# Two of eight tiles of an 8-bit rounding step finished on GpSimd instead of VectorE

## What is computed

```python
def _fp8_matmul(x2d, w):
    scale_x = jnp.maximum(jnp.max(jnp.abs(x2d)) / FP8_MAX, 1e-06)
    scale_w = jnp.maximum(jnp.max(jnp.abs(w)) / FP8_MAX, 1e-06)
    x8 = (x2d / scale_x).astype(jnp.float8_e4m3fn)
    w8 = (w / scale_w).astype(jnp.float8_e4m3fn)
    out = jnp.matmul(x8.astype(x2d.dtype), w8.astype(x2d.dtype).T)
    return out * (scale_x * scale_w)
h = _fp8_matmul(x2d, w_fc)               # 1024 x 1024
h = jnp.square(jax.nn.relu(h))
out = _fp8_matmul(h, w_proj)             # the second product; its h is rounded here
...
x = x + _L0_xattn_ref(_layernorm(x), ctx_512, ...)
x = x + _L0_ffn_ref(_layernorm(x), L0_ffn_w_fc, L0_ffn_w_proj)
x = x + _L1_xattn_ref(ctx_512, ctx_512, mask_SxS2_bk1, mask_BxS2_bf0, _layernorm(x), ...)
x = x + _L1_ffn_ref(_layernorm(x), ...)
```

## Time and profile before

| | |
|---|---|
| median of 3 runs | 506.76 us (506.63 to 507.72) |
| the profiled execution, whole time | 507.15 us |
| the profiled execution, from first to last instruction (its span) | 505.4 us |
| TensorE busy | 408.4 us, 81% of the span |
| VectorE busy | 353.0 us, 70% |
| ScalarE busy | 230.5 us, 46% |
| GpSimd busy | 201.5 us, 40% |
| TensorE's mean granted clock | 0.916 of 2.4 GHz |
| the chain that ended last | TensorE 54%, VectorE 26%, issue 7%, ScalarE 7%, GpSimd 4%, DMA 2% |

### The profile page before, as it was taken

How to read it: one execution, slowest core, us unless ns; L and a number is a source line. 1 busy time by engine, 2 the same in 40 slices (tenths; PEclk the granted TensorE clock), 3 DMA queues, 4 the chain that set the end, 5 groups by cost and what they waited for, 6 DMA issues and landing times.

```text
span 505.4 us, 5862 instructions
## 1 busy us (share of the span) xinstructions
PE 408.4 (81%) x1900; PEld 299.5 (59%) x1901; DVE 353.0 (70%) x765; ACT 230.5 (46%) x562; POOL 201.5 (40%) x150
## 2 busy tenths in 40 slices
PE   2956997999897988998989999929645058969997
PEld 2735776777786877777767888613423044524465
DVE  4996869868779699697786626474699966582322
ACT  1432653756666657666566550135792123311100
POOL 2582642644545627555566449771001110040000
PEclk9976999999999999999999999965895577979999
DMA  8633020020100200000200012000000000000011
GB/s 324 211 102 148 1 84 0 1 84 3 44 40 0 85 1 1 0 2 8 108 1 0 2 50 99 1 0 1 0 0 0 1 1 0 0 1 1 0 42 42
DMA packets 8941, 18.82 MB, mean 37 GB/s; under 512 B 2128, under 2 KB 6672, under 8 KB 7760
## 3 DMA queue, kind: packets, MB, share of 16 engines
q1 hardware_dynamic: 8912, 18.46, 10.6%
HBM read 17.40 MB, written 1.05 MB: 37 GB/s over the span
## 4 chain that ended last, share of the span: by engine, by line
PE 54%; DVE 26%; issue 7%; ACT 7%; POOL 4%; DMA 2%; SPq 0%; POOLq 0%; DVEq 0%; ACTq 0%
PE bank L1191 10%; PE bank L1196 5%; PE bank L1380 5%; PE bank L1398 5%; PE bank L1179 4%; PE bank L1090 4%; PE bank L1092 4%; PE bank L1091 4%; PE bank L1166 3%; POOL rot_low L387 2%; DVE negmax L806 2%; DVE tail_all L1011 2%; PE bank L1296 2%; PE bank L1085 2%; DVE qr L751 2%
## 5 line engine op out<-in xcount | busy, mean ns | idle before, releaser
L392 POOL TENSOR_TENSOR prob<-prob,rinv 128x512 f32<-128x512 f32 x64 | 77.0, 1203 | 104.5 <-DVE rinv L811 104.4
L549 ACT ACTIVATE prob<-bank,negmax 128x256 f32<-128x256 f32 x128 | 59.6, 470 | 53.2 <-DVE negmax L806 53.0
L1191 PE MATMUL bank<-probT,kva 128*128 128x256 f32 x256 | 68.2, 388 | 14.1 <-ACT probT L540 13.5
L1191 PEld LDWEIGHTS bank<-probT,kva 128*128 128x128 f32 x256 | 46.4, 189 | 27.9 <-ACT probT L540 20.8
L806 DVE TENSOR_REDUCE negmax<-bank 128x2 f32<-128x512 f32 x64 | 43.9, 685 | 18.3 <-PE bank L1166 18.2
L365 POOL TENSOR_TENSOR c_y<-c_ve,minus_half 128x4 f32<-128x4 f32 (+1 forms) x10 | 12.4, 1244 | 101.7 <-DVE c_ve L686 76.3
L540 ACT COPY probT<-bank 128x512 f32<-128x512 f32 x64 | 37.7, 588 | 22.5 <-PE bank L1179 21.4
L1380 PE MATMUL bank<-tailT,blobs 128*128 128x512 f32 (+1 forms) x96 | 45.7, 633 | 1.1 <-ACT tailT L479 0.8
L1166 PE MATMUL bank<-kvT,uT 128*128 128x256 f32 x256 | 45.7, 300 | 0.3
L1090 PE MATMUL bank<-xnT,w 128*128 128x512 f32 x96 | 40.3, 420 | 1.8 <-DVE rot_low L733 1.8
L1179 PE MATMUL bank<-ca,prob 128*128 128x128 f32 x256 | 38.8, 274 | 0.5 <-POOL prob L392 0.5
(11 more groups left out here) (205 smaller groups left out, 851.5 us busy)
## 6 DMA issues: line engine op xcount, KB each, us to landing
blobs<-in_blob SPq DMA_DIRECT2D x8, 1024.0 KB, 5.0
xs<-in_x SPq DMA_DIRECT2D x2, 512.0 KB, 4.0
ctxT<-in_ctx_t SPq DMA_DIRECT2D x1, 1024.0 KB, 13.2
xn<-in_w_fc_t SPq DMA_DIRECT2D x1, 1024.0 KB, 4.9
ctxT<-in_w_proj_t SPq DMA_DIRECT2D x1, 1024.0 KB, 5.4
out<-qk SPq DMA_DIRECT2D x8, 128.0 KB, 1.7
cb<-in_const_b SPq DMA_DIRECT2D x1, 768.0 KB, 9.1
blobs<-in_w_gate SPq DMA_DIRECT2D x1, 704.0 KB, 4.4
```

Source lines behind the costliest of these rows:

```text
L392: pool.tensor_tensor(p[:], p[:], rinv[:, n % PROBS, :].unsqueeze(2).to_broadcast([P, 2, S]), ALU.mult).then_inc(normed, 1)
L549: ins = act.activation(prob[n % PROBS][:, st, :], pS[n % 2][:, st * S:(st + 1) * S], ACT.Exp, bias=negmax[:, n % 2, st:st + 1], accum_out= ...
L1191: ins = pe.matmul(pV[b % 2][:, 0:S], kva[:, (2 * (2 * b + lt) + 1 - h) * DC:(2 * (2 * b + lt) + 1 - h) * DC + P], probT[n % 2][:, lt, :], ...
```

## The change

For tiles 2 and 5 (`ON_POOL`) VectorE does one pass in place of two: a `tensor_scalar` that only raises `hm` to at least 1.5 x 2^14, in place, in bfloat16 (`floor_ready`). GpSimd waits for that and does the two subtractions as `tensor_tensor`, the second after a wait on its own semaphore, and counts up a semaphore of its own, `h8_pool`. `h8_done(t)` says for each tile on which semaphore and number its readers wait; TensorE and ScalarE use it. VectorE's other tiles are as before.

```diff
+ON_POOL = (2, 5)
...
+        def h8_done(t):
+
+            if t in ON_POOL:
+                return h8_pool, ON_POOL.index(t) + 1
+            return h8_ready, sum(u not in ON_POOL for u in range(t + 1))
...
+            for i, t in enumerate(ON_POOL):
+                pool.wait_ge(floor_ready, i + 1)
+                in_order(pool.tensor_tensor(hv[t % 3], hm[t % 3], hv[t % 3], ALU.subtract))
+                pool.tensor_tensor(h8[:, :, t * P:(t + 1) * P], hm[t % 3].rearrange("p (f s) -> p f s", f=FT0),
+                                   hv[t % 3].rearrange("p (f s) -> p f s", f=FT0), ALU.subtract).then_inc(h8_pool, 1)
...
                 if t >= 3:
-                    act.wait_ge(h8_ready, t - 2)
+                    act.wait_ge(*h8_done(t - 3))
...
                 if t < NT:
                     dve.wait_ge(square_ready, t + 1)
+                if t in ON_POOL:
+                    dve.tensor_scalar(hm[t % 3], hm[t % 3], 1.5 * 2.0 ** 14, None, ALU.max).then_inc(floor_ready, 1)
+                elif t < NT:
                     dve.scalar_tensor_tensor(out=hv[t % 3], in0=hm[t % 3], scalar=1.5 * 2.0 ** 14, in1=hv[t % 3],
                                              op0=ALU.max, op1=ALU.subtract).then_inc(step_ready, 1)
-                    dve.wait_ge(step_ready, t + 1)
+                    dve.wait_ge(step_ready, h8_done(t)[1])
...
-                pe.wait_ge(h8_ready, t + 1)
+                pe.wait_ge(*h8_done(t))
```

More of the change, by code:

```diff
@@ L240, in build @@
         square_ready, h8_ready = sem("square_ready"), sem("h8_ready")
+        floor_ready, h8_pool = sem("floor_ready"), sem("h8_pool")
         z2_ready, step_ready = sem("z2_ready"), sem("step_ready")
```

## The result

The changed kernel takes 510.99 us (median of 7 runs, 509.17 to 512.24), the kernel before 506.76 (7 runs, 505.42 to 507.72). The ratio is 1.008 with an interval of 1.0054 to 1.0107: slower by 4 us. One execution further down, of the run e_one5, took 710.05 us at a mean granted clock of 0.558 and is left out of its numbers. The profiled execution took 511.45 us with a span of 509.7; before it was 507.15 and 505.4.

What follows compares the result with a forecast made beforehand. VectorE's unbroken list in the stage rounding h was taken as the bound; 3.56 us shed there, but waits for GpSimd leave it 2.89 late: 506.76 + 2.89 = 509.65, rounded 509.6, range 507.8 to 511.8.

Steps and rivals of the forecast that it cites:

- The bound: Stage in which h is rounded, up to the second layer's scores: VectorE's own list without a break, 3.25 us a tile.
- The exclusion: VectorE's and GpSimd's passes, both operands in SBUF, do not share time; rival of none or partial exclusion: 503.7 us, chance 0.09.
- The handover between VectorE's two passes: Tiles 3 and 6: GpSimd's second pass comes first; rival that VectorE keeps its turn: 508.2 us, chance 0.05.
- The step sizes: Tiles 2 and 5: one VectorE `tensor_scalar` (the floor) replaces two passes; 0.70 us, so 1.78 shed per tile.
- GpSimd's passes: Two `tensor_tensor` per tile in tiles 2 and 5: 2.37 us each alone, 2.21 behind VectorE's end.
- the rival: GpSimd slower on bfloat16 in tiles 2 and 5: 2.78 us per pass, 511.3 us; chance 0.10 together with a slower floor.
- ScalarE's copies: For tile 3, ahead of VectorE's first pass there: end at 371.57, just in time.
- Tiles 2 and 3: VectorE late by 1.81 us after tile 3: saved 1.78, lost 3.59 in waiting.
- Tiles 5 and 6: VectorE late by 2.89 us in all after tile 6.
- The rival of the held small instruction: L686 in `aggregate` held, GpSimd's second pass of tile 5 ahead of tile 6's first: 510.0 us; within the forecast's 0.73.
- The power: Queued behind GpSimd's passes of tile 5: done by 389.3, wanted only after 394, so it costs nothing.
- the allowance for the clock: Later stretches: where TensorE's clock is at 1.2 GHz can change when everything shifts; 1.5 us either way.

Runs made afterwards that it cites:

- e_one5: The changed kernel with tile 5 alone on GpSimd; 509.29 us, ratio 1.0032 to the kernel before.
- e_psum: The changed kernel with the value tile of tiles 3 and 6 in two PSUM banks, each VectorE pass in two halves; 504.72 us, ratio 0.9951.
- e_fill: The changed kernel with GpSimd's two subtractions per tile replaced by four fills with zeros, tiles 2 and 5 not rounded; 504.77 us, ratio 0.9955.
- the repeated comparison: The changed kernel once more without an edit, against the kernel before; 509.93 us against 507.23, ratio 1.0049.

## Why the prediction was right

The time came out at 510.99 where 509.6 was forecast, in the range of 507.8 to 511.8, and slower; in the stage it is slower by the mechanism named. By its steps:

- **The bound** was named rightly: VectorE's list is the stage. In the runs what its rows lost or gained is in the length of the stage (the sum for e_psum closes to 0.01 us).
- **The exclusion** of the earlier trace rows holds for bfloat16 operands too. e_psum and e_fill show it from both sides: move one of VectorE's operands, or take away GpSimd's reading, and it is gone.
- **The handover between VectorE's two passes** went to GpSimd in both places, as said; the second passes took 3.04 (about 3.3 was forecast). VectorE's passes ended 1.08 behind GpSimd's end, against the 1.09 read from the earlier trace rows.
- **The step sizes** were mis-sized: 0.42 us and not 0.70. The term from the earlier trace rows was too high; the estimate of 0.43 from the Trainium skill ("VectorE: DVE Perf Modes", the perf-mode tiers) was right, and the trace agrees with it. VectorE shed 2.06 us a tile (2.39 less the 0.33 from 371.57 to 371.90) and not 1.78.
- **GpSimd's passes** were mis-sized the other way than the rival had it: 2.14 alone and 1.99 behind VectorE's end, not 2.37 and 2.21 from the earlier trace rows. With one bfloat16 operand it is faster than L387 with two float32 ones, and not slower.
- **ScalarE's copies** for tile 3 came when they were forecast. They ended at 372.91 (the row below), and the stage began 1.33 us later than before, so that is 371.58 on the forecast's scale, which had 371.57. With the cheaper raising of the step sizes VectorE was ready at 372.76 and waited 0.18 us for them. That cost nothing, since the pass would have stood until 374.21 either way.

```profile
371.77 1.14 ACT L634 ACTIVATE ctxT<-cT,sc 128x1024 f32<-128x1024 f32 x1
```

- **Tiles 2 and 3** come to +1.07 instead of +1.81: 2.06 saved, and lost 0.18, 1.14 (2.35 less 1.21) and 1.81 (3.04 less 1.23). **Tiles 5 and 6** come to +0.53 instead of +1.08: 2.06 saved, and lost 0.77 (L700) and 1.81, which is 0.52 by the single rows.
- **The rival of the held small instruction** came true in its condition, and its price was wrong. I had GpSimd's second pass go ahead of tile 6's first; in the trace VectorE starts at 385.06 and GpSimd at 385.08, so L700 paid for the wait that the pass would have had anyway, and the two together cost 0.2 us more than the wait alone. Of the signs that were to show the forecast right, tile 6's first pass (2 to 2.8 us) was missed by it: it took 1.23.
- **The power** was late as said (388.24, 2.01 us), and nobody waited for it.

So the stage lost 1.60 us where 2.89 was forecast, and the first comparison shows 4.2. Two errors of opposite sign stand in a forecast that hit, and that they nearly cancel is luck: the stage was 1.3 us too dear by two sizes (0.28 us at each raising of the step sizes, 0.22 to 0.23 at each of GpSimd's four passes, less the 0.2 of L700), and the 2.7 us outside of it lay within the allowance for the clock and the spread, but were not foreseen as a sum. It is luck too that the scores begin at 393.38 where about 393.3 was named: 1.33 us of that stand ahead of the stage. And the distance from there to the end was not the same as before, but 1.4 us longer. Against the repeated comparison (1.0049, 2.5 us) the forecast is 0.4 us too high. The clock was named as what could move it by 1.5 us either way; rests of some 115 and some 116.3 us are what the runs showed of that.

## What to carry to other kernels

Ask of every pair of elementwise instructions on VectorE and GpSimd that is to run side by side where each operand lies: with two operands of VectorE in SBUF and GpSimd reading there, they took turns, and the tile that left VectorE cost more in held instructions (2.6 us at one place, 2.95 at the other) than it gave (2.06). Either one of VectorE's operands goes to PSUM (22.53 instead of 26.61 us for the stage, with GpSimd's share unchanged), or one-operand work stands in GpSimd's turn (24.93). Then compare the length of the changed stage, which repeats to 0.01 us, before the time of the kernel, which here lay between 505.94 and 511.79 us in twelve executions of one kernel. Look also where a profiled execution stands among the times of its kernel: one of the two shortest of twelve says little of the other ten.

## What I had not expected of the hardware

- A `tensor_scalar` on four float32 numbers per partition with one operand in SBUF is held by GpSimd: 0.94 us beside a subtraction and 0.74 beside a fill, which reads nothing, instead of 0.17. The passes with two operands were not held by the same fills. The Trainium skill ("SBUF — State Buffer", who interferes with whom) tells these apart: two SBUF inputs contend with a GpSimd instruction that reads SBUF, and a `tensor_scalar` in a two-port mode with any. The runs agree, as far as they show when an instruction is held; in which mode it ran no run here shows. Four numbers are enough.
- The `x2_tile` sum and its statistics (one operand in SBUF) took 0.47 and 0.43 us with and without GpSimd beside them.
- GpSimd's `tensor_tensor` over 128x1024 took 2.14 us with one bfloat16 input, against 2.37 at least with two float32 ones.
- A VectorE pass with its value tile in PSUM, in two halves of 512, took 1.29 us, against 1.23 for one of 1024 from SBUF: putting the operand there costs 0.06 us a pass.
